# Neighbourhood attention: keys, queries and output projections as two diagonal 64x64 tiles instead of one block diagonal 128x128 tile

## The reference

```python
# H, K, DIL = 8, 31, 2 ; DH = 64 // 8 ; x is (32, 512, 64) here
qkv = (x @ w_qkv + b_qkv).reshape(b, l, 3, H, DH)
q, k, v = (qkv[:, :, 0], qkv[:, :, 1], qkv[:, :, 2])
nbr = neighbor_indices(l, K, DIL)
kg = k[:, nbr]
vg = v[:, nbr]
attn = jnp.einsum('blhd,blkhd->blhk', q, kg) * DH ** (-0.5)
attn = jax.nn.softmax(attn, axis=-1)
out = jnp.einsum('blhk,blkhd->blhd', attn, vg).reshape(b, l, e)
return out @ w_proj + b_proj
```

## Time and profile before

| | |
|---|---|
| runs | 962.57 us median of 3 (961.24 to 964.74) |
| profiled execution | 959.21 us, span of the instructions 957.4 us |
| mean granted clock of TensorE | 0.931 of 2.4 GHz |
| TensorE matmul busy | 827.2 us, 86% of the span, 12656 records |
| TensorE weight load busy | 414.7 us, 43% |
| VectorE | 570.5 us, 60% |
| ScalarE | 469.8 us, 49% |
| GpSimd | 289.2 us, 30% |

### The profile page before, as it was taken

The page is one execution under the profiler, slowest core; times in us unless marked ns, Lnnn a source line. Parts: engine busy times, 40 slices in busy tenths (PEclk is TensorE's granted clock), DMA queues, the critical chain, the costliest instruction groups (busy, mean ns, idle before and its releaser), DMA issues. The chain is left out here.

```text
span 957.4 us, 28793 instructions
## 1 busy us (share of the span) xinstructions
PE 827.2 (86%) x12656; PEld 414.7 (43%) x12656; DVE 570.5 (60%) x831; ACT 469.8 (49%) x579; POOL 289.2 (30%) x286
## 2 busy tenths in 40 slices
PE   4796799999999987299999979298886599999996
PEld 2231477767767765022222212176663333333332
DVE  5446477757766765475857525086653147777776
ACT  2243476767767775154444453223332155555553
POOL 4034735334353431311222206533444160000000
PEclk9899799999999999699999979599988689999998
DMA  4200310010010010100000022312322101121110
GB/s 90 31 14 32 97 43 27 4 58 4 4 59 4 4 59 4 55 1 1 1 1 1 1 66 87 101 45 67 89 76 82 26 17 46 56 56 46 45 45 34
DMA packets 39775, 37.81 MB, mean 39 GB/s; under 512 B 21025, under 2 KB 25282, under 8 KB 39650
## 3 DMA queue, kind: packets, MB, share of 16 engines
q1 hardware_dynamic: 38578, 34.35, 12.8%
q10 hardware_dynamic: 1072, 1.60, 0.5%
HBM read 19.95 MB, written 7.60 MB: 29 GB/s over the span
## 5 line engine op out<-in xcount | busy, mean ns | idle before, releaser
L1914 ACT ACTIVATE se_a<-se_p,cols 128x512 f32<-128x512 f32 x128 | 92.7, 774 | 77.5 <-PE se_p L1867 77.5
L1191 DVE TENSOR_REDUCE na_rowmax<-na_ps 128x16 f32<-128x1024 f32 x64 | 78.1, 1220 | 76.8 <-PE na_ps L1067 76.8
L1483 DVE TENSOR_TENSOR me_gw<-me_pc,me_g 128x1024 f32<-128x1024 f32 x64 | 78.3, 1223 | 73.9 <-PE me_pc L1338 69.3
L1934 DVE SCALAR_TENSOR_TENSOR se_a<-se_p,cols,z 128x1024 f32<-128x1024 f32 x64 | 82.2, 1284 | 61.9 <-PE se_p L1877 61.9
L1379 ACT ACTIVATE me_g<-me_p,cols 128x1024 f32<-128x1024 f32 x64 | 71.3, 1114 | 83.9 <-PE me_p L1326 79.2
L925 POOL TENSOR_TENSOR z<-na_k,const 128x512 f32<-128x512 f32 x64 | 64.6, 1042 | 140.7 <-ACT na_k L1131 140.7
L496 POOL TENSOR_TENSOR n_sq<-h 128x512 f32<-128x512 f32 x64 | 68.6, 1077 | 110.3 <-DVE h L848 43.2
L531 POOL TENSOR_TENSOR z<-h,n_bc 128x512 f32<-128x512 f32 x62 | 78.4, 1280 | 24.4 <-DMA n_bc<-n_spread 24.3
L1194 DVE TENSOR_TENSOR na_e<-na_ps,na_rowmax 128x1024 f32<-128x1024 f32 x64 | 78.4, 1225 | 2.2
L1326 PE MATMUL me_p<-z,moe_w 64*64 64x512 f32 x512 | 72.4, 636 | 6.6 <-ACT me_g L1379 6.6
L1867 PE MATMUL se_p<-z,f_w 64*64 64x512 f32 x256 | 70.5, 618 | 4.9 <-DMA se_zswap<-z 4.0
(11 more groups left out here) (288 smaller groups left out, 1322.0 us busy)
## 6 DMA issues: line engine op xcount, KB each, us to landing
n_bc<-n_spread SPq DMA_DIRECT2D x128, 128.0 KB, 3.0
da_zswap<-z SPq DMA_DIRECT2D x32, 128.0 KB, 2.4
se_zswap<-z SPq DMA_DIRECT2D x32, 128.0 KB, 2.3
out<-se_rows SPq DMA_DIRECT2D x16, 256.0 KB, 2.1
n_spread<-n_rstd SPq DMA_DIRECT2D x13, 256.0 KB, 2.0
const<-in_const ACTq DMA_DIRECT2D x1, 712.0 KB, 6.4
const<-in_const ACTq DMA_DIRECT2D x1, 562.0 KB, 4.0
f_w<-in_L_ffn_W SPq DMA_DIRECT2D x4, 128.0 KB
```

Source lines behind the costliest of these rows:

```text
L1191: nc.vector.tensor_reduce(rowmax[b][:], scored, AX, ALU.max).then_inc(s_max, 1)
L1483: nc.vector.tensor_tensor(gw[at.k % 2][:], p_c[:], g[at.k % 2][:], ALU.mult).then_inc(s_gw, 1)
L1914: nc.scalar.activation(a1[at.k % 2][:, e2, :], hidden(at.n, e2)[:], ACT.Relu, scale=col(s, "f1_g1", 2 * ep + e2), bias=col(s, "f1_be1", 2 ...
L1934: nc.vector.scalar_tensor_tensor(out=a2[at.k % 2][:], in0=p_2[:], scalar=col(s, "f1_be2", ep), in1=s.f1_w[:, ep, :].unsqueeze(1).broadcast ...
```

## The change

A helper `by_batch` issues two matmuls, one for each sequence: rows 0 to 63 of the array with columns 0 to 63, and rows 64 to 127 with columns 64 to 127. Each reads its 64x64 quarter of the weight tile and its 64 partitions of the input, and writes its 64 partitions of `p_m`. The semaphore is raised by the second. Keys, queries and projection are issued so. All else is as before, and the buffers still hold the zero quarters.

```diff
+            def by_batch(w, x):
+                for b in range(2):
+                    hf = slice(64 * b, 64 * b + 64)
+                    mm = nc.tensor.matmul(p_m[hf, :], w[hf, hf], x[hf, :], start=True, stop=True, skip_group_check=True)
+                return mm
+
             def keys(at):
...
-                    nc.tensor.matmul(p_m[:], s.a0_wqk[:, 1, :], row(s.z, j), start=True, stop=True).then_inc(s_k, 1)
+                    by_batch(s.a0_wqk[:, 1, :], row(s.z, j)).then_inc(s_k, 1)
...
-                    nc.tensor.matmul(p_m[:], s.a0_wqk[:, 0, :], row(s.z, j), start=True, stop=True).then_inc(s_q, 1)
+                    by_batch(s.a0_wqk[:, 0, :], row(s.z, j)).then_inc(s_q, 1)
...
-                    nc.tensor.matmul(p_m[:], s.a0_wp.rearrange("p b d -> p (b d)"), ot[j % 2].rearrange("p a b -> p (a b)"), start=True, stop=True).then_inc(s_out, 1)
+                    by_batch(s.a0_wp.rearrange("p b d -> p (b d)"), ot[j % 2].rearrange("p a b -> p (a b)")).then_inc(s_out, 1)
```

## The result

| | before | change |
|---|---|---|
| median of 20 runs each | 961.08 us (958.15 to 968.98) | 969.59 us (961.12 to 976.95) |
| ratio, with its 95% interval | | 1.0077 [1.0052, 1.0103] |
| profiled execution | 959.21 us, span 957.4 | 972.18 us, span 970.4 |

The change is slower by 0.77%, some 7.4 us (5.0 to 9.9), where 2.9 us were forecast. The slowest run of the change, 976.95 us, was in the chip's slower state and is left out of the ratio. The medians lie 8.5 us apart, the means without that run 7.4. Against the 962.57 us of the forecast that ratio gives 970.0 us; the range ended at 968.5. The 20 runs of the change also lie further apart than those of before.

A forecast was written before the change was run, and what follows sets the result against it. TensorE was taken to bound the neighbourhood attention. Group prices of 2.25 + 1.50 - 0.70 = 3.05 us, with -0.1 and -0.05 outside them, gave +2.9 us on a median of 962.57: 965.5 us, range 961.5 to 968.5.

The forecast's parts named there:

- What bounds the kernel: Neighbourhood attention: TensorE sets the pace, busy 267 of 291 us; only the even values wait for ScalarE.
- Tiles side by side, passes give nothing back: Keys, queries, projection: the two diagonal tiles overlap, 1.01 us per group; half-zero passes take their columns' time either way.
- Rival 1: Two tiles writing one PSUM bank take turns: 0.84 us for each of 48 operations, about 1009 us; chance 0.12.
- Output projection +0.15, queries +0.10, keys -0.05: Us per group from tile shape changes and weight loads, over 15 projections, 15 queries and 14 keys: 3.05 us.
- The first keys, the first queries, the last projection: Operations outside the 3.05 us: first keys -0.1 us at the lower clock, first queries 0, last projection -0.05.
- The instruction stream: Three more matmuls a pair add 6 matmul records and 6 weight loads: taken as 0, at most 1.0 us in all.
- the sum: All priced groups of the neighbourhood attention together: +2.9 us, with nothing to hide it.
- rival 3: TensorE pauses inside groups that nothing releases may shift, one or two us either way; chance 0.06 on the fast side.
- Rival 2: No slower: the even values' 0.50 us wait for ScalarE absorbs the added 0.25; -0.9 us, 961.7 us; chance 0.12.
- the line of 0.3%: The smallest difference a measurement of this kernel can tell from no change: about 0.3%, 2.9 us.

The follow-up runs named there:

- where the supply plays no part: Weighted values of two query tiles sent as one matmul, in the kernel before and in the change; first scores to stage's end 291.8 against 295.1 us.
- the shift by 128: The change with 64 tiny unread matmuls (128 instructions) ahead of the first keys; ratio to the kernel before 1.0043 [1.0013, 1.0073], stage 292.8 us.
- keys_only: Only the keys as two diagonal tiles, queries and projection one matmul each, against the kernel before; ratio 0.9987 [0.9961, 1.0012], stage 289.2 us.

## Why the prediction was right or wrong

- *What bounds the kernel.* Right: TensorE sets the pace, and what was added to it came through in full.
- *Tiles side by side, passes give nothing back.* Right: 1.00 us for the projection and the queries, 1.01 for the keys. Rival 1 falls, in which each group would have taken 1.8 us (its time was added up wrong, too: 962.57, 2.9 and 40 give 1005 to 1006 us, and the 1009 has the 2.9 twice). The rule of the Trainium skill (TensorEngine Tiling (Array Packing), section Restrictions and Gotchas) on row tiles and one bank does not hold in this case. Here the tiles write different partitions of the bank; two row tiles on the same partitions were not tried.
- *Output projection +0.15, queries +0.10, keys -0.05.* Right, per group and in sum: the stage is 3.3 us longer where the supply plays no part and 2.9 in the shift by 128; alone the projection gave +3.3 (1.1 of it pauses), the queries +1.4 and the keys -0.7.
- *The first keys, the first queries, the last projection.* The first keys gained the 0.1 us. The rest is too small to see.
- *The instruction stream "I take 0 for it", with 10 ns a record as its upper bound.* This is the step that failed. The bound was taken from the rate at which TensorE works off instructions, but they must also arrive, 256 at a time, and the stage is so dense that blocks come late already before: 4.1 us of idle time in that profile. The change had 9.5 and 10.8 us: 5.4 and 6.7 us more idle time in the stage, and 3.2 to 3.5 us more of the runs' time at full clock than the sum has, in place of 0 and at most 1.0. The row for it stood in the prediction, filed as rival 3 with a chance of 0.06 and on the fast side alone. A pause inside a group, with no semaphore, should have been asked what it waits for.
- *Rival 2.* Wrong: the even values' waits for ScalarE were there afterwards too (0.34 us at 260.86; 1.5 us in 5 waits over the stage, before 2.0 in 7), and the stage became longer.
- *The numbers.* 2.9 us were forecast and 7.4 measured, and the forecast sat on the line of 0.3% where the result is clear of it. The range ended 1.5 us short of 970.0.

No kernel here beats the one before beyond doubt. keys_only is the one that should, by 0.8 us: its stage is 0.7 us shorter, its ratio 0.9987 [0.9961, 1.0012].

## What to carry to other kernels

Splitting a block diagonal float32 tile into its diagonal halves saved no pass in this kernel, and it cost a change of shape (0.09 us) on each side whose neighbour had the old shape, and a bare weight load (0.06 us) for the neighbour behind; it paid (0.05 us) only between neighbours of other shapes. Price a group by the distance between starts, with the same neighbours, taken from anywhere in the trace: that gave each group to 0.01 us. And where TensorE runs some 65 instructions a microsecond, count instructions as well as work: look for pauses within a group that nothing releases, and whether they stand a multiple of 256 instructions apart.

## What the runs showed of the hardware

- TensorE's instructions arrive in blocks of 256 (16 KB); the first of a block started 2.2 us at the least after the block's transfer began (2.18 the lowest of 130), and dense code that reached the block's end sooner waited, 4 to 11 us in a stage of 290.
- A change that alters no work (two matmuls of 256 columns for one of 512) cost 0.49% [0.18, 0.80], up to half of it perhaps by the clock, and 128 instructions of no use, at the right place, took 6 to 9 us off the stage of a slower kernel (some 4 us off its runs at full clock).
- Two 64*64 tiles of different rows that write different partitions of one PSUM bank ran side by side: 1.00 us for four passes of 512 columns, as two column tiles take.
